# Reciprocal root of the head norms: two ScalarE activations instead of a ScalarE root and a VectorE reciprocal

## Chip, cores, metric

One core of a Trainium2 chip. The metric is the device time of one execution in microseconds (us); a change is judged by the median of several runs against the kernel before.

## What is computed

64 sequences of 128 tokens with 128 channels pass through a gated cross attention (16 heads of 8 channels, 120 context rows each), then through a gated block of causal self attention and four experts. The change sits in the self attention, in the norm of each query and key head:

```python
def _rms(x, w):
    return x * jax.lax.rsqrt(jnp.mean(x * x, axis=-1, keepdims=True) + EPS) * w
h = _rms(x, n1_w)
heads = lambda w_: (h @ w_.T).reshape(B, T, HEADS, HD).transpose(0, 2, 1, 3)
q = _rms(heads(wq), qn_w)        # HD = 8
k = _rms(heads(wk), kn_w)
```

The experts use GELU and SiLU, both attentions a softmax.

## The kernel before

The 64 sequences are worked off in 16 groups of four. A group passes five parts, one per step of a software pipeline: N (layer norm and projections of the cross attention), A (cross attention), B (projections and head norms of the self attention), D (self attention, gates, first expert layers), M (rest of the experts, output). So each step works on five groups at once. Four ramp steps fill the pipeline, a hardware loop runs the full step 12 times (t = 3 to 14), and four tail steps empty it.

What each engine does in a step is a list written out by hand (`SCHEDULE` and the ramp and tail lists); all five engine programs walk the same list and take from it only their own entries, in its order. No engine reorders: an instruction whose operand is late holds up all that its engine has behind it. Buffers and PSUM banks are guarded by semaphores; a bank counts one `filled` by the producer and one `drained` by the reader.

The entries around the change, in the order of the full step:

- ("B","squares"): GpSimd squares the queries and keys of a group; ("B","sums"): VectorE adds them by head into `hs`, 128 values per partition.
- ("A","base"), three product entries of D, ("D","nT",0): ScalarE copies `onT` (line 958).
- ("B","root"): ScalarE waits for `hs` and writes `hr`, the root of the mean square plus epsilon (line 905).
- ("M","e2_l2",0) and ("M","e2_l2",1): TensorE multiplies (line 1400), ScalarE applies Gelu (line 947). Between them ("D","wo",0): TensorE (line 1375), then VectorE adds into x2 (line 1147).
- ("B","scale"): VectorE waits for `hr`, takes the reciprocal (line 1070) and multiplies queries and keys by it (line 1072). It stands behind ("D","wo",0) on VectorE.
- estimate("A",3): TensorE (line 1305) fills four banks, VectorE takes their maxima (line 1091, out `mpadA`). values("D",3): TensorE (line 1362), ScalarE copies `oT` (line 955). ("M","e3_up",0) and (1) on TensorE and ScalarE.
- ("D","oT",1): TensorE transposes `oT` (line 1224), VectorE divides by the softmax sums (`rden` line 1130, `on` line 1132); ("D","nT",1): TensorE transposes `on`.
- later in the step ("B","qT") and ("B","kT"): transposes of the scaled queries and keys.

The exponentials of both attentions are line 951, those of the gates line 914; SiLU is made with Tanh (line 940). Ahead of some activations the trace shows an instruction ACT_TABLE_LOAD under the line of the activation behind it; the kernel's source doesn't write these.

In the third ramp step "root" stands between exponentials, in the fourth between a copy of `onT` and one of `oT`; in the last step that has it (t = 16) it stands ahead of the copy of `onT`.

Of the kernel before, what the change touches and what calls it, by code (L numbers as in the profile page):

```python
# [28 lines left out]
ACT = mybir.ActivationFunctionType  # L29
AX = mybir.AxisListType  # L30

P = 128
# [3 lines left out]
H = 16  # L36
HD = 8
# [4 lines left out]
G = 4  # L42
# [112 lines left out]
def slot_of(part, b, c):  # L155

    return (("AD".index(part) * G + b) * NT + c) % SLOTS
# [263 lines left out]
def build(nc, x, ctxT, weights, vcols, rows, out):  # L421
    ctx = ExitStack()
    with ctx:
        def sb(name, shape, dt=F32):
            return ctx.enter_context(nc.sbuf_tensor(name, shape, dt))

        def sem(name):
            return ctx.enter_context(nc.semaphore(name))
# [19 lines left out]
        rms_eps = sb("rms_eps", [P, G])  # L448
# [49 lines left out]
        rsA = sb("rsA", [P, G])  # L498
        rB = sb("rB", [P, 2, G])
        vrB = sb("vrB", [P, G])  # L500
        hs, hr = sb("hs", [P, 2 * H * G]), sb("hr", [P, 2 * H * G])
        ssM, msM, rM = sb("ssM", [P, G]), sb("msM", [P, G]), sb("rM", [P, G])
        lg = sb("lg", [P, 8, G, E])
        sm = sb("sm", [P, 5, G])
# [19 lines left out]
        a_stats, a_rstd, xn_ready, x1_base = (sem(n) for n in ("a_stats", "a_rstd", "xn_ready", "x1_base"))  # L524

        x1_copied, b_stats, b_pow, b_rs, hb_ready = (sem(n) for n in ("x1_copied", "b_stats", "b_pow", "b_rs", "hb_ready"))
        x2_ready, sq_ready, hs_ready, root_ready, hr_ready, qk_ready = (sem(n) for n in ("x2_ready", "sq_ready", "hs_ready", "root_ready", "hr_ready", "qk_ready"))
        y_ready = sem("y_ready")

        m_sq, m_ms, m_r, xf_ready, kept = (sem(n) for n in ("m_sq", "m_ms", "m_r", "xf_ready", "kept"))  # L530
# [22 lines left out]
        def half_of_maxima(p, half, b):  # L553

            at = (2 * half + b) * P
            return qd[p][M_ROW:M_ROW + 1, :, :, at:at + P].rearrange("p j c n -> p (j c) n").bitcast(F32)

        def half_source(p, half, b):

            return (mTl if half else mTr)[p][b * H:(b + 1) * H, :].bitcast(F32)  # L560

        def maxima_by_act(st, part, work):

            return (part, work, st.group(part, work)) in (("A", "mH", 0), ("B", "mH", 0), ("D", "mL", 0))
# [268 lines left out]
        def _(act):  # L833
# [8 lines left out]
            def clear_queries(p, first, last, done):  # L842

                nc.scalar.activation(qd[p][:, first:last].rearrange("p j c t -> p (j c t)"),
                                     one[:].to_broadcast([P, (last - first) * NT * TOK]), ACT.Copy, scale=0.0).then_inc(done, 1)
# [4 lines left out]
            def queries_or_keys(st, part, to, o, **affine):  # L850

                key = (part, {"N": o, "B": o + "T"}[part], 0)
                width = G * keys[to] if o == "k" else TOK
                bank = psum[st.bank[key]][:, 0:width]
                act.wait_ge(filled[st.bank[key]], st.fills(*key))
                nc.scalar.activation((qTb if o == "q" else kTb)[to][:], bank, ACT.Identity, **affine).then_inc(cast_ready[to], 1)
                n = uses_of_split(st, part)
                if not isinstance(n, int) or n > 0:

                    act.wait_ge(split_stored[o], n * USE_STORED)  # L860
                nc.scalar.activation(split[o][:, 0, 0:width], bank, ACT.Identity, **affine).then_inc(high_ready[o], 1)

            def step(st):
                for part, work, index in st.works:
                    key, g = (part, work, index), st.group(part, work, index)
# [31 lines left out]
                    elif (part, work) == ("B", "v"):  # L897
                        if st.first("B"):
                            act.wait_ge(vb_cleared, 1)
                        act.wait_ge(full, st.fills(*key))  # L900
                        nc.scalar.activation(V["B"][:, :, 0:HD],
                                             bank[:].rearrange("p (n d) -> p n d", d=HD), ACT.Copy).then_inc(done, 1)
                    elif (part, work) == ("B", "root"):
                        act.wait_ge(hs_ready, g + 1)
                        nc.scalar.activation(hr[:], hs[:], ACT.Sqrt, bias=rms_eps[:, 0:1], scale=1.0 / HD).then_inc(root_ready, 1)
                    elif (part, work) == ("B", "qT"):
                        if st.first("B"):
                            act.wait_ge(bias_ready, 3)
                        queries_or_keys(st, "B", "B", "q", scale=qns[:])
                    elif (part, work) == ("B", "kT"):  # L910
                        queries_or_keys(st, "B", "B", "k", scale=col["kn"])
                    elif (part, work, index) == ("D", "gates", 0):
                        act.wait_ge(gate_step, g * GATE_STEPS + 3)
                        nc.scalar.activation(lg[:, 3], lg[:, 2], ACT.Exp).then_inc(gate_exp, 1)
                    elif work == "mT":
                        act.wait_ge(full, st.fills(*key))
                        nc.scalar.activation(mTr[OP[part]][:], bank[0:G * H, 0:P], ACT.Copy).then_inc(done, 1)
                    elif work in HALVES:
                        p, half = OP[part], HALVES.index(work)
                        act.wait_ge(full, st.fills(*key))  # L920
                        nc.scalar.activation(mTl[p][:] if half else mTr[p][0:G * H // 2, :], bank[0:G * H // 2, 0:P],
                                             ACT.Copy).then_inc(done, 1)
                        if maxima_by_act(st, part, work):
                            if (part, work) == ("A", "mH"):
                                act.wait_ge(a_cleared, A_CLEARED)
                            elif (part, work) == ("B", "mH"):
                                act.wait_ge(b_cleared, B_CLEARED)
                            act.wait_ge(done, st.fills(*key))
                            for b in range(2):
                                act.dma_start(half_of_maxima(p, half, b), half_source(p, half, b)).then_inc(half_loaded[p][half], 16)  # L930
                        if st.parts == "N":
                            clear_queries("B", 0, HT // 2, b_cleared)
                    elif work == "fill" and index[0] == "e1_w1":

                        if index[1]:

                            for b, n in st.drains([("D", "fill", ("e1_w1", index[1] - 1))]):
                                act.wait_ge(drained[b], n)
                        act.wait_ge(full, st.fills(*key))
                        nc.scalar.activation(th, bank[:], ACT.Tanh, scale=0.5).then_inc(silu_tanh, 1)  # L940
                    elif work == "fill" and index[0] in HID_AT:
                        if index == ("e0_up", 0):

                            for b, n in st.drains([("D", "fill", ("e1_w1", 1)), ("D", "fill", ("e1_w2", 1))]):
                                act.wait_ge(drained[b], n)
                        act.wait_ge(full, st.fills(*key))
                        nc.scalar.activation(hid[:, HID_AT[index[0]] + index[1], :], bank[:], ACT.Gelu).then_inc(done, 1)  # L947
                    elif work == "s2":
                        k = keys[OP[part]]
                        act.wait_ge(full, st.fills(*key))  # L950
                        nc.scalar.activation(probs[0:k, slot_of(part, *index), :], bank[0:k, :], ACT.Exp,  # L951
                                             scale=SCALE if part == "A" else 1.0).then_inc(done, 1)
                    elif work == "pv" and key in st.bank:
                        act.wait_ge(full, st.fills(*key))
                        nc.scalar.activation(oT[:], bank[:], ACT.Copy).then_inc(done, 1)  # L955
                    elif work == "nT":
                        act.wait_ge(full, st.fills(*key))
                        nc.scalar.activation(onT[:], bank[:, 0:2 * P], ACT.Copy).then_inc(done, 1)  # L958

            run_steps(act, step)  # L960

        @block.vector
        def _(dve):
# [32 lines left out]
            def step(st):  # L996
                for part, work, index in st.works:
                    key, g = (part, work, index), st.group(part, work, index)
# [68 lines left out]
                            .then_inc(hs_ready, 1)  # L1067
                    elif (part, work) == ("B", "scale"):
                        dve.wait_ge(root_ready, g + 1)
                        nc.vector.reciprocal(hr[:], hr[:]).then_inc(hr_ready, 1)  # L1070
                        dve.wait_ge(hr_ready, g + 1)
                        nc.vector.tensor_tensor(
                            qk[:].rearrange("p b (h d) -> p (b h) d", d=HD), qk[:].rearrange("p b (h d) -> p (b h) d", d=HD),
                            hr[:].rearrange("p (n a) -> p n a", a=1).to_broadcast([P, 2 * H * G, HD]), ALU.mult)\
# [33 lines left out]
                    elif work == "fill" and index[0] == "down":  # L1108
                        e = index[1]
                        n = DOWNS.index(e)  # L1110
# [346 lines left out]
```

## Time and profile before

| | |
|---|---|
| median of 3 runs | 1075.44 us (1074.19 to 1075.52) |
| profiled execution | 1072.52 us, span 1070.7 us |
| TensorE | 1004.9 us busy, 94% of the span |
| VectorE | 789.2 us, 74% |
| ScalarE | 736.1 us, 69% |
| GpSimd | 337.8 us, 32% |
| granted TensorE clock, mean | 0.987 |
| table loads on ScalarE, by line | 836: 1, 905: 16, 914: 2, 947: 30, 951: 29 (78 in all; none at line 940) |

The shares are averages over the whole span. What a change in one place does is read from the chain of waits and from the timeline of that place. A step of the loop takes 62.7 us.

### The profile page before, as it was taken

Reading aid. Unit: us, or ns where it says so; the run is one execution under the profiler, and the core shown is the slowest. Engines: PE = TensorE matmul, PEld = TensorE weight load, DVE = VectorE, ACT = ScalarE, POOL = GpSimd, SP = SyncE. Lnnn points to the kernel's source line nnn. Section 1 sums busy time; section 2 is a strip of 40 time slices with the busy share of each in tenths; the row PEclk is TensorE's granted clock in tenths of the full one; section 3 lists DMA queues with packets and bytes.
Section 4 is the critical chain, followed back from the end, with each engine's and each line's share of the span. In section 5 each row is a group of like instructions: output and inputs, shape, how many; then the busy total and the mean of one; then the engine's idle time right before and its main releaser. Section 6 shows DMA issues by size and latency. Waiting matters only on the chain.

```text
span 1070.7 us, 26205 instructions
## 1 busy us (share of the span) xinstructions
PE 1004.9 (94%) x8649; PEld 626.3 (58%) x8649; DVE 789.2 (74%) x2172; ACT 736.1 (69%) x1334; POOL 337.8 (32%) x463
## 2 busy tenths in 40 slices
PE   6678799999999999999999999999999999999898
PEld 5445456566665656666565666656566665655565
DVE  8667777877787787778778777877877777774723
ACT  6466677676777767677776767777676777767453
POOL 5615134051513405151240515124051512404130
PEclk9989899999999999999999999999999999999999
DMA  7433432233343233434323343432234343221200
GB/s 233 134 106 130 136 112 93 90 102 127 115 142 111 90 92 103 127 115 140 109 92 92 106 127 115 136 109 93 90 111 127 115 135 109 82 67 62 69 1 20
DMA packets 77317, 114.28 MB, mean 107 GB/s; under 512 B 7776, under 2 KB 40160, under 8 KB 77152
## 3 DMA queue, kind: packets, MB, share of 16 engines
q1 hardware_dynamic: 76800, 111.53, 33.0%
q10 hardware_dynamic: 480, 2.26, 0.6%
q8 instruction: 23, 0.38, 0.1%
q14 instruction: 14, 0.11, 0.0%
HBM read 58.97 MB, written 53.74 MB: 105 GB/s over the span
## 4 chain that ended last, share of the span: by engine, by line
PE 64%; DVE 15%; ACT 11%; issue 7%; DMA 1%; SPq 1%; POOL 0%; DVEq 0%; ACTq 0%
PE ps_pv L1362 9%; PE ps_w L1388 9%; PE ps_s2a L1341 7%; PE ps_s2b L1341 5%; PE ps_s2a L1400 5%; PE ps_s2b L1407 4%; PE ps_t L1224 4%; ACT probs L951 4%; PE ps_w L1407 3%; DVE mpadB L1091 3%; PE ps_w L1273 3%; DVE mpadA L1091 3%; PE ps_t L1375 2%; PE ps_w L1224 2%; PE ps_w L1305 2%
## 5 line engine op out<-in xcount | busy, mean ns | idle before, releaser
L951 ACT ACTIVATE probs<-ps_s2a 120x512 f32<-120x512 f32 (+1 forms) x256 | 153.4, 599 | 73.1 <-PE ps_s2a L1341 64.7
L1091 DVE TENSOR_REDUCE mpadB<-ps_w 128x4 f32<-128x512 f32 x240 | 148.8, 684 | 24.9 <-PE ps_w L1305 24.9
L1091 DVE TENSOR_REDUCE mpadA<-ps_w 128x4 f32<-128x480 f32 x224 | 131.5, 651 | 38.0 <-PE ps_w L1305 38.0
L951 ACT ACTIVATE probs<-ps_s2b 120x512 f32<-120x512 f32 (+1 forms) x256 | 153.6, 600 | 0.0
L818 POOL TENSOR_SCALAR_AFFINE_SELECT probs<-probs 128x1024 f32<-128x1024 f32 x128 | 139.8, 1092 | 0.0
L1388 PE MATMUL ps_w<-W,hid 128*128 128x96 f32 x976 | 122.5, 279 | 1.0 <-DVE split_k L985 0.9
L1388 PEld LDWEIGHTS ps_w<-W,hid 128*128 128x128 f32 x976 | 114.9, 193 | 10.4 <-issue 4.9
L786 POOL TENSOR_TENSOR rB<-vrB,neg_half 128x4 f32<-128x4 f32 x16 | 16.1, 1007 | 207.2 <-DVE veB L978 207.2
L1341 PE MATMUL ps_s2a<-qdA,kstA 128*120 128x512 f32 x128 | 68.7, 537 | 7.0 <-ACT probs L951 3.1
L1400 PE MATMUL ps_s2a<-hid,W 128*128 128x512 f32 x152 | 74.4, 604 | 0.0
L1120 DVE SCALAR_TENSOR_TENSOR ym<-ps_w,gates,ym 128x96 f32<-128x96 f32 x184 | 45.7, 311 | 38.5 <-PE ps_w L1388 38.5
L955 ACT ACTIVATE oT<-ps_pv 128x512 f32<-128x512 f32 x64 | 38.2, 598 | 50.6 <-PE ps_pv L1362 50.6
L1341 PE MATMUL ps_s2a<-qdB,kstB 128*128 128x512 f32 x128 | 65.0, 508 | 7.4 <-ACT probs L951 1.9
L947 ACT ACTIVATE hid<-ps_s2a 128x512 f32<-128x512 f32 x73 | 43.7, 598 | 40.0 <-PE ps_s2a L1400 30.9
L1362 PE MATMUL ps_pv<-probs,VA 120*18 120x128 f32 x2048 | 68.5, 274 | 0.1
L1362 PE MATMUL ps_pv<-probs,VB 128*18 128x128 f32 x2048 | 68.5, 274 | 0.0
L1362 PEld LDWEIGHTS ps_pv<-probs,VA 120*18 120x18 f32 x2048 | 50.5, 98 | 23.4 <-issue 23.1
L817 POOL TENSOR_TENSOR tick<-one 128x1 f32<-128x1 f32 x128 | 24.9, 194 | 118.8 <-ACT probs L951 114.7
L1362 PEld LDWEIGHTS ps_pv<-probs,VB 128*18 128x18 f32 x2048 | 50.5, 97 | 17.1 <-issue 16.8
L958 ACT ACTIVATE onT<-ps_t 128x256 f32<-128x256 f32 x64 | 24.5, 383 | 50.4 <-PE ps_t L1224 50.4
L1341 PE MATMUL ps_s2b<-qdA,kstA 128*120 128x512 f32 x128 | 58.7, 458 | 0.0
L825 POOL TENSOR_TENSOR ym<-yb,one 128x128 f32<-128x128 f32 x16 | 6.4, 398 | 164.6 <-DMA out_x<-ym 164.6
(279 smaller groups left out, 2166.7 us busy)
## 6 DMA issues: line engine op xcount, KB each, us to landing
scratch_Aq<-split_q SPq DMA_DIRECT2D x48, 256.0 KB, 2.4
qdA<-scratch_Aq SPq DMA_DIRECT2D x64, 192.0 KB
scratch_Bq<-split_q SPq DMA_DIRECT2D x48, 256.0 KB, 2.4
scratch_Bk<-split_k SPq DMA_DIRECT2D x48, 256.0 KB, 2.9
qdB<-scratch_Bq SPq DMA_DIRECT2D x64, 192.0 KB
kstB<-scratch_Bk SPq DMA_DIRECT2D x64, 192.0 KB
scratch_Ak<-split_k SPq DMA_DIRECT2D x48, 240.0 KB, 2.3
kstA<-scratch_Ak SPq DMA_DIRECT2D x64, 180.0 KB
```

Of the source, the lines that this page charges most:

```text
L818: pool.affine_select(out=tile, in_=tile, compare_op=ALU.is_ge, fill=0.0, base=0, pattern=[[0, 2 * HT], [1, P]], channel_multiplier=-1).the ...
L947: nc.scalar.activation(hid[:, HID_AT[index[0]] + index[1], :], bank[:], ACT.Gelu).then_inc(done, 1)
L951: nc.scalar.activation(probs[0:k, slot_of(part, *index), :], bank[0:k, :], ACT.Exp, scale=SCALE if part == "A" else 1.0).then_inc(done, 1)
L955: nc.scalar.activation(oT[:], bank[:], ACT.Copy).then_inc(done, 1)
L1091: nc.vector.tensor_reduce(pair[:, :, c, b % 2] if halves else mneg[p][:, :, c, b], bank[:, 0:HT * k].rearrange("p (h k) -> p h k", h=HT), ...
L1120: ins = nc.vector.scalar_tensor_tensor(out=ym[:, b, KEEP:P], in0=bank[:, b * UP:(b + 1) * UP], scalar=gates[:, b, e:e + 1], in1=y[:, b, KE ...
L1224: ins = nc.tensor.transpose(psum[st.bank[key]][:, b * P:(b + 1) * P], of(b), identf[:])
L1341: mm(o, kst[p][:, c, b * k:(b + 1) * k], qd[p][:, :, c, b * P:(b + 1) * P], start=True, stop=True).then_inc(done, 1)
L1362: ins = mm(psum[st.bank[last]][32 * j:32 * j + VS, at:at + P], VB[p][0:k, first:first + VS], probs[0:k, slot_of(part, b, c), j * P:(j + 1) ...
L1388: ins = mm(bank[:, b * UP:(b + 1) * UP], hid[:, HID_AT[h] + k, b * P:(b + 1) * P], w[f"down{index[1]}"][:, k * UP:(k + 1) * UP], start=k = ...
L1400: ins = mm(bank[:], w[name][:, k * HID + c * P:k * HID + (c + 1) * P], hid[:, HID_AT[h] + k, :], start=k == 0, stop=k == chunks[-1])
L1407: mm(bank[:], w[name][:, c * P:(c + 1) * P], xfT[:], start=True, stop=True).then_inc(done, 1)
```

## The change

ScalarE takes the logarithm of the mean square plus epsilon into a new buffer `hl`, waits for its own result, and takes exp(-0.5 x) of it into `hr`. VectorE's reciprocal and its wait go; the multiplication follows directly on the wait for `hr`.

```diff
-        hs, hr = sb("hs", [P, 2 * H * G]), sb("hr", [P, 2 * H * G])
+        hs, hl, hr = (sb(n, [P, 2 * H * G]) for n in ("hs", "hl", "hr"))
...
                     elif (part, work) == ("B", "root"):
                         act.wait_ge(hs_ready, g + 1)
-                        nc.scalar.activation(hr[:], hs[:], ACT.Sqrt, bias=rms_eps[:, 0:1], scale=1.0 / HD).then_inc(root_ready, 1)
+                        nc.scalar.activation(hl[:], hs[:], ACT.Ln, bias=rms_eps[:, 0:1], scale=1.0 / HD).then_inc(log_ready, 1)
+                        act.wait_ge(log_ready, g + 1)
+                        nc.scalar.activation(hr[:], hl[:], ACT.Exp, scale=-0.5).then_inc(root_ready, 1)
...
                         dve.wait_ge(root_ready, g + 1)
-                        nc.vector.reciprocal(hr[:], hr[:]).then_inc(hr_ready, 1)
-                        dve.wait_ge(hr_ready, g + 1)
                         nc.vector.tensor_tensor(
```

The semaphore `hr_ready` is replaced by `log_ready`.

## Rows read from the trace of the kernel before

**Rows 1.** Page, chain that ended last, shares of the span by engine.

```profile
PE 64%; DVE 15%; ACT 11%; issue 7%; DMA 1%; SPq 1%; POOL 0%; DVEq 0%; ACTq 0%
```

**Rows 2.** Groups by line, ScalarE: count | busy us, mean ns | idle before us.

```profile
L951 ACT ACTIVATE probs<-ps_s2a 120x512 f32<-120x512 f32 (+1 forms) x256 | 153.4, 599 | 73.1 <-PE ps_s2a L1341 64.7 <-issue 1.2
...
L951 ACT ACT_TABLE_LOAD x29 | 37.2, 1283 | 0.5
...
L905 ACT ACT_TABLE_LOAD x16 | 20.5, 1283 | 0.3
...
L905 ACT ACTIVATE hr<-hs,rms_eps 128x128 f32<-128x128 f32 x16 | 6.4, 401 | 0.2
...
L914 ACT ACTIVATE lg<-lg 128x16 f32<-128x16 f32 x16 | 3.3, 209 | 0.8 <-DVE lg L1175 0.7
```

**Rows 3.** Line 1070 alone: duration ns min/median/max, first and last start us.

```profile
L1070 DVE RECIPROCAL hr<-hr x16: 941/942/953, 64.1 to 979.2; 128x128 f32<-128x128 f32 x16
```

**Rows 4.** Chain of waits in one loop step: start us, us on the chain, what.

```profile
356.89 0.36 DVE x L1147
357.25 0.87 DVE hr L1070
...
358.14 0.85 DVE qk L1072
...
359.28 2.21 DVE mpadA L1091 x4
...
361.54 0.36 DVE rden L1130
...
362.41 0.44 PE ps_t L1224 x2
```

**Rows 5.** Timeline of that step, ScalarE and TensorE: start us, us, instruction [idle before].

```profile
355.15 1.28 ACT L905 ACT_TABLE_LOAD   x1
...
356.87 1.28 ACT L947 ACT_TABLE_LOAD   x1
...
358.16 0.60 ACT L947 ACTIVATE hid<-ps_s2a 128x512 f32<-128x512 f32 x1
358.53 0.38 PE L1305 MATMUL ps_w<-kdA,qTbA 32*128 32x480 bf16 x4
...
359.84 1.12 PE L1400 MATMUL ps_s2a<-hid,W 128*128 128x512 f32 x2
359.97 0.60 ACT L955 ACTIVATE oT<-ps_pv 128x512 f32<-128x512 f32 x1 [0.73 <-PE ps_pv L1362]
360.80 0.60 PE L1224 MATMUL ps_t<-identf,oT 128*128 128x128 f32 x4
...
361.24 1.02 PE L1400 MATMUL ps_s2b<-hid,W 128*128 128x512 f32 x2
```

**Rows 6.** Timeline, same loop step and the one before: VectorE waiting for TensorE.

```profile
327.28 0.60 PE L1224 MATMUL ps_t<-identf,oT 128*128 128x128 f32 x4
...
327.91 0.36 DVE L1130 RECIPROCAL rden<-ps_t 128x32 f32<-128x32 f32 x1 [1.05 <-PE ps_t L1224]
...
343.60 0.38 PE L1305 MATMUL ps_w<-kdA,qTbA 32*128 32x480 bf16 x4
...
343.99 2.35 DVE L1091 TENSOR_REDUCE mpadA<-ps_w 128x4 f32<-128x480 f32 x4 [1.85 <-PE ps_w L1305]
```

**Rows 7.** Chain of waits, third ramp step.

```profile
62.40 1.28 ACT L905
...
65.11 1.24 DVE qk L1072
```

**Rows 8.** Chain of waits, fourth ramp step.

```profile
106.23 0.61 ACT oT L955
```

**Rows 9.** Last step with the change (t = 16): timeline, then chain of waits.

```profile
979.10 0.36 ACT L958 ACTIVATE onT<-ps_t 128x256 f32<-128x256 f32 x1
...
982.14 0.60 ACT hid L947
```

More of the change, by code:

```diff
@@ L526, in build @@
         x1_copied, b_stats, b_pow, b_rs, hb_ready = (sem(n) for n in ("x1_copied", "b_stats", "b_pow", "b_rs", "hb_ready"))
-        x2_ready, sq_ready, hs_ready, root_ready, hr_ready, qk_ready = (sem(n) for n in ("x2_ready", "sq_ready", "hs_ready", "root_ready", "hr_ready", "qk_ready"))
+        x2_ready, sq_ready, hs_ready, log_ready, root_ready, qk_ready = (sem(n) for n in ("x2_ready", "sq_ready", "hs_ready", "log_ready", "root_ready", "qk_ready"))
         y_ready = sem("y_ready")
```

## Prediction

> **What bounds the kernel now.** I read the page's chain first: two thirds of it are TensorE, the rest mostly VectorE and ScalarE in short pieces [rows 1]. So the kernel isn't bound by one engine's total but by TensorE's order with small gaps in it, and a change counts where it moves such a gap. Then the groups by line on ScalarE, which give the prices of table loads and activations [rows 2], and the reciprocal's own row [rows 3]. Then the chain of waits around one root in the loop [rows 4] and the timeline of the same place [rows 5]. The twelve loop steps and the step t = 15 have the same pattern to within some hundredths of a microsecond (I looked at seven of these 13), so one is worked out and multiplied by 13. The three other places with a root (third and fourth ramp step, t = 16) are read one by one [rows 7 to 9].
>
> In the loop step the reader is to see that the reciprocal and the multiplication by it lie on the chain: the addition of line 1147 at 356.89, the reciprocal from 357.25, the multiplication from 358.14, four maxima from 359.28, the division by the softmax sums from 361.54, and the transposes of `on` at 362.41 [rows 4]. But TensorE works through this stretch too. It fills the banks of the maxima from 358.53, multiplies for e3_up 0 from 359.84, transposes `oT` from 360.80 and multiplies for e3_up 1 from 361.24 [rows 5]. So the only gap of TensorE that this VectorE chain makes is the one ahead of 362.41, and it is small.
>
> **What goes on VectorE.** 16 reciprocals of 942 ns [rows 3], 15.1 us in all. In the loop step the multiplication could follow at 357.27 in place of 358.14, 0.87 us earlier, if `hr` is there by then. The first maximum then waits for TensorE: elsewhere line 1091 starts 0.39 us after the first matmul of line 1305 [rows 6], which here gives 358.53 + 0.39 = 358.92, 0.36 us earlier than 359.28. Four maxima end at 361.13. The division waits for the transposes of `oT`: 0.63 us after their start in [rows 6], so 360.80 + 0.63 = 361.43 in place of 361.54. That leaves 0.11 us for the transposes of `on`. TensorE can take it: the two matmuls of line 1400 end at 361.24 + 1.02 = 362.26 by the timeline, and groups overlap at their ends by some 0.16 us there (the transposes run from 360.80 to 361.40, the matmuls start at 361.24) [rows 5], so TensorE is free from about 362.10. Of 0.87 us taken off VectorE, 0.11 us reach the end of the step, 13 x 0.11 = 1.4 us in all. The rest is covered by TensorE's own work.
>
> **What comes on ScalarE, without the tables.** Ln takes the form of the root (128 columns, a bias from memory): 401 ns [rows 2]. The Exp behind it has 128 columns and no bias from memory. Its price isn't in the trace; it lies between the 16-column Exp of the gates at 209 ns and the root at 401 ns [rows 2]. The slope of ScalarE from this trace's wide activations puts it near 300 ns: 599 ns at 512 columns against 209 at 16 is 0.79 ns per column [rows 2], and 209 + 112 x 0.79 = 297. I take 0.30 us. The new wait on `log_ready` has behind it the Gelus of line 947 and the copy of `oT`; it costs a hop of 0.02 us, as between root and reciprocal today.
>
> **What happens to the tables.** This decides the sign. Each table load is 1.28 us [rows 2]. A loop step has five: root, Gelu, Exp, Gelu, Exp. Today the root stands behind the exponentials of part D and ahead of the Gelus, with a load ahead of it at 355.15 and one ahead of Gelu at 356.87 [rows 5]. The trace shows where functions share a table: Tanh, Copy and Identity stand behind Exp (and, in the tail, Tanh behind Gelu) without a load. It shows also where they don't: Sqrt after Exp, Gelu after Sqrt, Exp after Gelu each pay one. Ln occurs nowhere, so no row can say whether Ln and Exp stand in one table. The loads are placed function by function, immediately ahead of the first activation that misses its table; none of them shows that an earlier load was chosen for a function further on. Exp is now always served by a table that also served Tanh. If Ln brings a table of its own, as each of the three curves Exp, Sqrt and Gelu does, the order becomes load, Ln, load, Exp, load, Gelu: one load more than now. I take this as the likeliest, though only by a little.
>
> The Trainium skill speaks for the other way. "ScalarE: Activation LUTs", section "Table sets: the hidden batching unit", lists a set that holds both exp and ln and counts one load for ln followed by exp. "ScalarE activation tables: per-element evaluation and per-set limits", section "Table sets in the compiler and the runtime", says the loads are placed by the longest run that one set can serve. By that the change takes a load away rather than adding one, which is the second rival below. No row of this trace shows Ln, so the rule is neither borne out nor refuted.
>
> **The sum, with one load more.** Loop step on ScalarE: load to 356.43, Ln to 356.85, load 356.87 to 358.15, Exp 358.16 to 358.46, load to 359.76, Gelus at 359.78 and 360.27, copy of `oT` at 360.76, ending 361.36; today that copy ends at 360.57 [rows 5]. Everything behind the root moves by 1.28 + 0.30 = 1.6 us, of which 0.73 us is idle time ahead of the copy of `oT` [rows 5] and is absorbed. On VectorE the multiplication starts at 358.50 in place of 358.14, the maxima end near 361.85. On TensorE e3_up 0 needs the bank that the first Gelu frees at 360.38, so it starts at 360.42 (now 359.84); the transposes of `oT` start at 361.40, the division at 361.40 + 0.63 = 362.03 (now 361.54), and the transposes of `on` come 0.87 us behind it as now [rows 4], at 362.90: 0.48 us later than 362.41. So 13 x 0.48 = 6.2 us.
>
> Third ramp step: load 62.40 to 63.68, Ln to 64.10, load to 65.40, Exp to 65.71; the multiplication starts at 65.74 in place of 65.11 [rows 7], 0.6 us late on the chain. The exponentials behind it already pay a load today, so they lose only 0.3. Fourth ramp step: load and Exp (1.6 us) come ahead of the copy of `oT`, which moves from 106.23 [rows 8] to 107.43: 1.2 us. The load for the next exponentials goes, but TensorE waits there for the maxima's transfer, which has moved with it. Step t = 16: the copy of `onT` ends near 981.05 in place of 979.46 [rows 9]; line 1375, line 1400 and the second Gelu follow, that Gelu at 983.35 in place of 982.14: 1.2 us.
>
> Sum: 6.2 + 0.6 + 1.2 + 1.2 = 9.2 us. The profiled execution was 1072.52 us, the median of the runs 1075.44; the difference of 2.9 us is that between executions of one kernel, and I add the sum to the median: 1084.6 us. Bounds of this case: if Exp is nearer 209 or 401 ns each place moves by 0.1 us (1.6 us in all). If the late Gelus also hold e3_up 1, or the ScalarE backlog runs on into the transposes of the queries, a loop step loses 0.8 us instead of 0.48, 4 us more. If half of the loop's delay is taken up in later gaps, 3 to 4 us less. So 1079 to 1090 us.
>
> **Rivals.** *Ln's table also holds Exp, and it is loaded only when Ln comes* (chance 0.15). Then the root costs a load, Ln, Exp, and Gelu its load, as now. `hr` is there at 356.85 + 0.02 + 0.30 = 357.17, before VectorE has finished line 1147 at 357.25. The gelus move by 0.3 us, inside the 0.73 us of idle time ahead of the copy of `oT` [rows 5]. The loop gains 1.4 us as worked out; in the third ramp step the multiplication starts at 64.45 in place of 65.11, 0.7 us; the other two places gain nothing. Together 2.1 us: 1073.3 us, faster or no change about evenly. For it speaks that Tanh is found in more than one table; against it that no other curve of this kernel is.
>
> *The table with both functions is loaded at the start of part D's exponentials and serves them, Ln and Exp.* The chance is 0.22. A load goes in each step, 16 x 1.28 = 20.5 us of ScalarE's work [rows 2]. In the loop the multiplication still has to wait for line 1147, and TensorE doesn't wait for ScalarE between 355 and 361, so the gain is again 1.4 us. In the third ramp step Ln follows the exponentials directly and the multiplication comes when VectorE is free, near 63.85: 1.26 us. Together 2.7 us: 1072.7 us. It is what the longest-run rule of the Trainium skill cited above would do. This is the case on the other side of my forecast. It decides for faster as soon as one load serves Ln and Exp.
>
> *One load more, but the delay is hidden* (chance 0.06). If e3_up 0 were allowed its bank earlier or the backlog ended in the idle time of ScalarE, only the three single places would pay, some 3 us less the 1.4 us of the reciprocal: 1077 us. Against it: the copy of `oT` has 0.73 us of slack [rows 5] and 1.6 us come on top.
>
> **How the numbers follow.** The forecast has a chance of 0.57, the rivals 0.15, 0.22 and 0.06. A change of about 0.2% (2.2 us) is what a measurement of this kernel can tell from none. The first rival lies on this bound, the second a little beyond it, the third is near it on the slow side. Slower: 0.57 less a small part, plus a part of the third rival, 0.59. Faster: most of the second rival and a third of the first, 0.22. Same: 0.19. The range has to hold both signs: 1071.5 to 1090 us; the forecast's own range is 1079 to 1090.
>
> **What would show it.** The count of table loads decides first: 78 now. In the forecast they become 92 (one more in the 13 like steps and at t = 16; in the third and fourth ramp step the Exp of the root saves the load of the next exponentials). In the first rival they become 76, in the second 60 to 64. Next the start of the multiplication behind line 1147: directly behind it (0.02 us) in both rivals, 1.2 us later in the forecast. Next the idle time ahead of the copy of `oT`: gone in the forecast, 0.4 us or more otherwise. Last the start of the transposes of `on` after the addition of line 1147: 5.5 us now, 6.0 in the forecast, 5.4 in the rivals. The prediction is wrong if Ln and Exp share a load; its size is wrong if Exp or the Gelus' bank waits are off.

## The result

The changed kernel took 1087.39 us (median, 1084.63 to 1089.87) against 1074.82 us before; the ratio is 1.0118, 95% interval 1.0087 to 1.0148. On a second chip run it took 1082.57 us against 1074.11 us, ratio 1.0080 (1.0060 to 1.0100). So it is slower, by 8.5 to 12.6 us (0.8% to 1.2%). No load serves both Ln and Exp in this program: each of the 16 roots now pays two loads.

The groups by line of the changed kernel on ScalarE, with count, busy us, mean ns and idle before; the answer to [rows 2]:

```profile
L949 ACT ACT_TABLE_LOAD x30 | 38.5, 1283 | 0.6
L953 ACT ACT_TABLE_LOAD x27 | 34.6, 1283 | 0.5
L905 ACT ACT_TABLE_LOAD x16 | 20.5, 1283 | 0.3
L907 ACT ACT_TABLE_LOAD x16 | 20.5, 1283 | 0.3
L905 ACT ACTIVATE hl<-hs,rms_eps 128x128 f32<-128x128 f32 x16 | 6.4, 402 | 0.2
L907 ACT ACTIVATE hr<-hl 128x128 f32<-128x128 f32 x16 | 5.0, 309 | 0.2
```

With two loads for the gates and one at the start that makes 92, where there were 78. Line 953 (the softmax exponentials, line 951 before) has 27 in place of 29: in the third and fourth ramp step the root's Exp leaves its table standing for them. The Trainium skill ("ScalarE: Activation LUTs", section "Table sets: the hidden batching unit") counts one load for ln followed by exp; here the trace shows a load at each of the 16 Exps behind a Ln, and the measurement decides.

The page's chain by engine, the answer to [rows 1]: VectorE fell from 15% to 9% and ScalarE rose from 11% to 16%.

```profile
PE 63%; ACT 16%; DVE 9%; issue 9%; DMA 1%; SPq 1%; POOL 0%; ACTq 0%; DVEq 0%
```

One loop step of the changed kernel, chain of waits (start us, us, what), the answer to [rows 4]:

```profile
360.87 1.28 ACT L905
...
362.16 0.40 ACT hl L905
...
363.87 0.31 ACT hr L907
...
365.50 0.60 ACT hid L949
...
366.15 1.12 PE ps_s2a L1400 x2
367.27 0.59 PE ps_t L1224 x4
...
368.76 0.44 PE ps_t L1224 x2
```

And its timeline, the answer to [rows 5]:

```profile
362.60 0.36 DVE L1147 TENSOR_TENSOR x<-ps_t,x 128x192 f32<-128x192 f32 x1 [1.75 <-PE ps_t L1375]
...
364.20 1.28 ACT L949 ACT_TABLE_LOAD   x1
364.22 1.23 DVE L1072 TENSOR_TENSOR qk<-qk,hr 128x1024 f32<-128x1024 f32 x1 [1.26 <-ACT hr L907]
...
365.50 0.60 ACT L949 ACTIVATE hid<-ps_s2a 128x512 f32<-128x512 f32 x1
365.99 0.59 ACT L949 ACTIVATE hid<-ps_s2b 128x512 f32<-128x512 f32 x1
...
366.15 1.12 PE L1400 MATMUL ps_s2a<-hid,W 128*128 128x512 f32 x2 [0.53 <-ACT hid L949]
366.47 0.60 ACT L957 ACTIVATE oT<-ps_pv 128x512 f32<-128x512 f32 x1
367.19 0.42 PEld L1224 LDWEIGHTS ps_t<-identf,oT 128*128 128x128 f32 x4 [0.75 <-issue]
367.20 0.65 PE L1224 MATMUL ps_t<-identf,oT 128*128 128x128 f32 x4
...
367.89 0.36 DVE L1130 RECIPROCAL rden<-ps_t 128x32 f32<-128x32 f32 x1 [0.18 <-PE ps_t L1224]
```

The chain no longer runs through the multiplication and the maxima on VectorE; of VectorE's work only the division is left on it, and VectorE stands idle 0.18 us ahead of that, waiting for TensorE. It goes from the two loads of the root and the load of Gelu through the Gelu to the bank that e3_up 0 waits for: TensorE now stands idle 0.53 us ahead of it, where it had no idle time. The 0.73 us of slack ahead of the copy of `oT` [rows 5] are gone. The transposes of `on` come 6.16 us behind the addition of line 1147 in place of 5.52. From multiplication to multiplication a loop step takes (933.04 - 174.69) / 12 = 63.20 us; before it was (921.16 - 170.31) / 12 = 62.57 (the text ahead of the prediction gives it as 62.7). The rows at both ends of the changed kernel's twelve steps:

```profile
174.69 1.22 DVE L1072 TENSOR_TENSOR qk<-qk,hr 128x1024 f32<-128x1024 f32 x1 [1.26 <-ACT hr L907]
...
933.04 1.23 DVE L1072 TENSOR_TENSOR qk<-qk,hr 128x1024 f32<-128x1024 f32 x1 [1.26 <-ACT hr L907]
```

### The profile page after: what moved, and what is told of

The parts are those of the page before. It is cut to its first block, busy times and chain, and to the rows that moved or that the text cites. A ratio compares the mean times of both kernels' runs of the same rounds, so it can differ in the third digit from the quotient of the medians.

```text
span 1087.1 us, 26219 instructions
## 1 busy us (share of the span) xinstructions
PE 1013.0 (93%) x8649; PEld 629.1 (58%) x8649; DVE 776.6 (71%) x2156; ACT 756.3 (70%) x1364; POOL 338.5 (31%) x463
## 4 chain that ended last, share of the span: by engine, by line
PE 63%; ACT 16%; DVE 9%; issue 9%; DMA 1%; SPq 1%; POOL 0%; ACTq 0%; DVEq 0%
PE ps_pv L1362 9%; PE ps_w L1388 9%; PE ps_s2a L1341 7%; PE ps_s2b L1341 5%; PE ps_t L1224 5%; PE ps_s2b L1407 4%; PE ps_s2a L1400 4%; ACT probs L953 4%; PE ps_w L1407 3%; DVE mpadB L1091 3%; PE ps_w L1273 3%; PE ps_w L1224 2%; PE ps_w L1305 2%; PE ps_w L1301 2%; PE ps_t L1375 2%
## 5 line engine op out<-in xcount | busy, mean ns | idle before, releaser
L1375 PEld LDWEIGHTS ps_t<-W,onT 128*128 128x128 f32 x256 | 38.4, 193 | 33.8 <-issue 20.1
```

The lines of the kernel that those rows point to most:

```text
L1375: ins = mm(bank[:, s * n:(s + 1) * n], onT[:, s * P:(s + 1) * P], w["Wo"] if part == "A" else w["wo"], start=True, stop=True)
```

## The experiments

Periods below are always taken so, from the multiplication at t = 3 to the one at t = 15.

### The reciprocal alone

```diff
-                        nc.vector.reciprocal(hr[:], hr[:]).then_inc(hr_ready, 1)
-                        dve.wait_ge(hr_ready, g + 1)
```

> The kernel before with VectorE's reciprocal left out (queries and keys are multiplied by the root itself). ScalarE and its table loads are as before, 78. This prices the reciprocal alone. Theory (TensorE covers it): in the loop the transposes of `on` come 5.4 us behind the addition of line 1147 in place of 5.5, 13 x 0.11 = 1.4 us less, and about 1 us less in the third ramp step: 1072 to 1073 us. Rival (the reciprocal's 0.87 us on the chain is worth its whole length): 13 x 0.87 = 11 us less, 1063 us.

Measured: 1073.11 us against 1074.11, ratio 0.9992 (0.9977 to 1.0007). The loop step is (922.37 - 172.69) / 12 = 62.47 us, 0.10 us less than before. In this timeline the first maximum waits for TensorE, as worked out:

```profile
359.79 0.36 DVE L1145 TENSOR_TENSOR x<-ps_t,x 128x192 f32<-128x192 f32 x1 [1.75 <-PE ps_t L1373]
360.06 1.21 DVE L1070 TENSOR_TENSOR qk<-qk,hr 128x1024 f32<-128x1024 f32 x1
...
361.84 2.35 DVE L1089 TENSOR_REDUCE mpadA<-ps_w 128x4 f32<-128x480 f32 x4 [0.56 <-PE ps_w L1303]
...
363.70 0.60 PE L1222 MATMUL ps_t<-identf,oT 128*128 128x128 f32 x4
...
364.34 0.36 DVE L1128 RECIPROCAL rden<-ps_t 128x32 f32<-128x32 f32 x1
```

The rival of 11 us is excluded. 0.94 us of VectorE per step, 0.87 of them on the chain of waits, were worth 0.10 us. In the third ramp step the multiplication came 1.73 us behind the root's load (66.64 - 64.91) in place of 2.71, so the 1 us expected there was found. The time of the whole kernel shows neither: its interval goes from 2.5 us less to 0.8 us more.

### Two activations without a table load

```diff
-                        nc.scalar.activation(hl[:], hs[:], ACT.Ln, ...
+                        nc.scalar.activation(hl[:], hs[:], ACT.Exp, ...
```

> The changed kernel with Exp in place of Ln (the logarithm is left out), so that no table has to be loaded at the root at all. Same count of activations and the same wait on the own result as in the changed kernel; 60 to 64 table loads in place of 92. Theory (the table loads are the whole loss): 1072 to 1073 us, some 2.5 us under the kernel before, and the transposes of `on` 5.4 us behind line 1147. Rival (the second activation and the wait on the own result cost too, 0.3 us in each of 16 places): 1077 us or more.

Measured: 1072.10 us against 1074.11, ratio 0.9979 (0.9962 to 0.9996), with 60 loads. The loop step is (918.90 - 169.22) / 12 = 62.47 us, the same as without the reciprocal alone. So in the loop a second activation and its wait cost nothing where no load stands at the root, and a load less on ScalarE brings nothing there either. That the second activation is free behind two loads isn't shown by this; the next experiment bears on it. What separates this kernel from the changed one (10.5 us in these medians) is the table loads.

### One load more, reciprocal kept

```diff
                         nc.scalar.activation(hr[:], hs[:], ACT.Sqrt, ...).then_inc(root_ready, 1)
+                        nc.scalar.activation(atick[:], one[:], ACT.Exp)
```

> The kernel before (root and reciprocal kept) with an Exp of one column behind the root, whose result nobody reads. It adds a table load at 14 places, as the changed kernel does, without making `hr` later. Theory of the bank and the copy (the Gelus and the copy of `oT` come 1.5 us later and hold TensorE): about 0.5 us in each of 13 steps, 1080 to 1083 us. Rival (the loss comes through VectorE, whose multiplication starts 0.36 us later than before): the extra load behind the root would cost nothing, 1075 us.

Measured: 1081.98 us against 1074.11, ratio 1.0080 (1.0061 to 1.0100), the same ratio as the changed kernel beside it. The loop step is (928.36 - 170.84) / 12 = 63.13 us, 0.56 us more than before. This timeline shows VectorE's multiplication 2.99 us behind the root's load (360.35 - 357.36), exactly as before (358.14 - 355.15), and TensorE idle all the same:

```profile
357.36 1.28 ACT L906 ACT_TABLE_LOAD   x1
...
359.08 1.28 ACT L907 ACT_TABLE_LOAD   x1
...
360.35 1.22 DVE L1074 TENSOR_TENSOR qk<-qk,hr 128x1024 f32<-128x1024 f32 x1
...
360.58 1.28 ACT L949 ACT_TABLE_LOAD   x1
...
362.52 1.12 PE L1402 MATMUL ps_s2a<-hid,W 128*128 128x512 f32 x2 [0.41 <-ACT hid L949]
```

So the loss comes by the late Gelus and the late copy of `oT`, not by the late `hr`: 0.56 of the 0.63 us are there with `hr` in time. The remaining 0.07 us fit the root's Exp of 309 ns, where this kernel has one of 203; that isn't tested by itself. Nor is it separated which of the two, Gelu or copy, costs how much.

### The changed kernel again

> The changed kernel again, for a second profile and more times. The loop step took 63.20 us in its first profile and 62.57 before, 0.63 us more; the entry to the loop was 4.0 us late and the tail 4.3 us, with a granted clock of 0.67 between 70 and 80 us and of 0.52 between 1030 and 1040 us. Theory (the loop is the same in each execution, and what varies is the clock in ramp and tail): the loop step is again 63.2 us within 0.05, and the total goes with the mean clock, about 2 us less for 0.003 more. Rival (the loss in ramp and tail is fixed by the table loads): entry and tail are late by the same 4 us again whatever the clock.

Measured: 1082.57 us, ratio 1.0080 (1.0060 to 1.0100). The loop step is (933.39 - 174.85) / 12 = 63.21 us. The theory holds for the loop and for the tail. In the first profile TensorE stood idle 1.75 us before 1024.64 and ran mostly at its lower level of 1.2 GHz after it; in the second it stood idle for the same 1.75 us before 1025.03 and kept 2.4 GHz. The stretches (busy us and count of PE, PEld, DVE, ACT, POOL, then granted clock, DMA share, GB/s), first and second profile:

```profile
1030.00:1040.00 10.00, 9.54 (x79) 5.37 (x78) 0.00 (x0) 5.75 (x11) 6.03 (x10) 0.52 0.01 2
```

```profile
1030.00:1040.00 10.00, 9.49 (x117) 5.43 (x117) 0.78 (x2) 7.86 (x14) 7.62 (x13) 1.00 0.01 2
```

79 matmuls against 117 in the same time. From the multiplication at t = 16 to the end it was 94.2 us and 89.9 us. The entry to the loop, on the other hand, was as late as the first time (174.85 against 174.69), which speaks for the rival there. In the first four executions the mean clock and the time went together: 0.986 and 1084.63 us, 0.983 and 1085.80, 0.980 and 1088.99, 0.978 and 1089.87.

### Loop only, ramp and tail only

```diff
+                        if st.parts == PARTS:        # the second kernel: !=
                             ... Ln, wait, Exp
+                        else:
+                            ... Sqrt; and on VectorE the reciprocal
```

> Ln and Exp in the 12 loop steps only; root and reciprocal as before in the ramp and the tail. Theory (the loop step is 0.63 us longer whatever stands around it): 12 x 0.63 = 7.5 us over the kernel before, period of the loop 63.2 us. Rival (the loop carries less and the ramp's lost clock the rest): under 5 us over.

> Ln and Exp in the ramp and the tail only (4 places), root and reciprocal as before in the loop. Theory by the prediction's terms: 0.6 us at t = 15, 0.6 and 1.2 in the third and fourth ramp step, up to 1.2 at t = 16, together 3 to 3.6 us over the kernel before. Rival (where the changed kernel's first profile has 8 us in ramp and tail, a lower granted clock is part of every execution with the later root): 6 to 8 us over.

Measured: loop only 1081.42 us against 1075.13, ratio 1.0054 (1.0035 to 1.0072); ramp and tail only 1077.76 us, ratio 1.0024 (1.0005 to 1.0042). In microseconds 5.8 (3.8 to 7.7) and 2.6 (0.5 to 4.5), together 8.4, as the changed kernel has on the second run. For the loop the interval alone doesn't exclude the rival of under 5 us; the trace does. Between the root's loads of t = 3 and t = 15 lie 758.3 us in the first kernel (the multiplication of a step with Ln comes 3.35 us behind its first load, one with a root 2.99 us) and 750.7 us in the second; before it was 750.9, so the loop alone carries 7.4 us. For ramp and tail the rival of 6 to 8 us is excluded.

The loop-only kernel, whose ramp is that of before, had its multiplication of the fourth ramp step at 113.51 us, where before had 109.28 and the changed kernel 112.63. So the 4 us by which the changed kernel enters the loop late in its profile aren't the change's alone: the ramp varies by as much between executions, and before's profile was an early one.

### Matmuls in the ramp's idle times

```diff
+            BUSY = {(1, "B", "hT"): 34, (1, "B", "qT"): 24, (2, "B", "hT"): 16, (2, "N", "xT"): 40}
+                for _ in range(k):     # ahead of the wait for hb, qk or xn
+                    mm(psum[st.bank[key]][:, 0:P], identf[:], identf[:], start=True, stop=True)
```

> The changed kernel with matmuls whose result is overwritten, on TensorE in four idle times of the ramp (34 ahead of the first transposes of hb, 24 ahead of the first of the queries, 16 and 40 in the fourth ramp step), in the bank that is filled next. Theory (the spread between executions and the rest of the loss in the ramp are TensorE's clock after idle times): the granted clock stays at 1.0 between 50 and 130 us and the kernel is 3 to 6 us faster than the changed kernel, near 1078 us. Rival (TensorE isn't what the ramp waits for): no more than 1 us faster.

> The kernel before with the same matmuls in the idle times of the ramp (34, 20, 16 and 40). Theory (clock after idle times): 3 to 6 us faster than the kernel before, 1068 to 1071 us, and thereby faster than both kernels. Rival: within 1 us of the kernel before.

Measured: 1092.61 us for the changed kernel, 1081.19 us for the one before, ratios 1.0148 (1.0116 to 1.0179) and 1.0053 (1.0034 to 1.0072). The theory failed in both, and nobody had expected a loss: the kernels got slower, though their mean clock rose to 0.994 and 0.993. The chain of the kernel before with these matmuls shows why, they had become what everything waits for:

```profile
47.93 7.86 PE ps_w L1230 x68
```

34 calls are 68 instructions and 7.86 us, for an idle time of 4.4 us (4.43 ahead of the transposes of `hb` at 51.72 in the kernel before). Hence the same with about half the counts, 18, 10 (12 in the changed kernel), 8 and 20:

> The kernel before with fewer matmuls in the ramp's idle times (18, 10, 8 and 20 in place of 34, 20, 16 and 40): each call of 128 columns had taken 0.23 us, twice what was assumed, so that the larger counts ran 3.5, 2.2, 1.6 and 4.2 us past the operand they were to wait for. Theory (clock after idle times): now they end with the idle times, the granted clock stays near 1.0 from 50 to 130 us, and the kernel is 3 to 5 us faster than before, 1070 to 1072 us. Rival (the ramp waits on VectorE, ScalarE and transfers, not on TensorE's clock): within 1 us of before.

> The changed kernel with 18, 12, 8 and 20 such matmuls. Theory: 3 to 6 us faster than the changed kernel, 1077 to 1080 us, with less spread between executions, and 7.5 to 9 us over the kernel before with its own such matmuls, since the loop's loss of 0.63 us a step isn't one of clock. Rival: as slow as the changed kernel, 1082 to 1087 us.

Measured: the kernel before with the matmuls took 1069.73 us against 1073.50, ratio 0.9963 (0.9947 to 0.9979). That is 4.0 us less (2.3 to 5.7), as the theory had it, and beats both kernels. The changed kernel with them took 1082.97 us, ratio to before 1.0067 (1.0043 to 1.0091), which can't be told from the 1.0080 of its second run without them: here the rival came true. Stretches of the kernel before without them, and with them:

```profile
50.00:60.00 10.00, 7.33 (x33) 4.85 (x37) 1.12 (x4) 6.09 (x14) 3.23 (x3) 0.68 0.12 34
60.00:70.00 10.00, 6.92 (x78) 4.67 (x70) 7.03 (x21) 8.60 (x14) 2.19 (x3) 0.83 0.01 2
```

```profile
50.00:60.00 10.00, 8.59 (x74) 6.04 (x72) 1.72 (x5) 6.36 (x14) 4.53 (x4) 1.00 0.10 30
60.00:70.00 10.00, 7.10 (x70) 5.33 (x70) 7.48 (x23) 9.02 (x14) 1.40 (x2) 1.00 0.08 29
```

In the changed kernel with them the clock held up to 70 us and then fell: TensorE stood idle 2.67 us ahead of 71.14 and was granted 0.53 in the stretch from 70 to 80 us. Its timeline and stretch:

```profile
71.14 0.61 PE L1316 MATMUL ps_w<-causal_k,causal_q 32*128 32x512 bf16 x4 [2.67 <-DVE split_k L987]
...
73.24 1.91 PE L1377 MATMUL ps_pv<-probs,VA 120*18 120x128 f32 x32
```

```profile
70.00:80.00 10.00, 8.39 (x72) 4.40 (x76) 7.11 (x17) 2.56 (x6) 0.00 (x0) 0.53 0.84 272
```

The kernel before with them stood idle for the same 2.67 us at the same place and was granted 1.00 over 70 to 80 us:

```profile
70.27 0.40 PE L1316 MATMUL ps_w<-causal_k,causal_q 32*128 32x512 bf16 x4 [2.67 <-DVE split_k L985]
```

So the filling works as far as it reaches, and only if the clock isn't lost at the next idle time that is left. Why the kernel before kept it there in its profile and the changed one didn't isn't settled; the length of the idle time isn't the reason.

## Why the prediction was right

**The bound.** Right: TensorE's order with small gaps. It was the reading of TensorE beside the chain that priced the reciprocal. The chain alone gives 0.87 us a step, the timeline 0.11, and the kernel without it 0.10.

**The tables.** Right in sign and count: 92 loads forecast and found. The choice itself wasn't proven by any row of before. What stood for it were three curves with a table each and loads that looked no further than the next activation, and a chance of 0.57 was fair to that: that it came so was in part luck. Why Exp got a load of its own behind Ln, the trace doesn't say; it only shows the loads. The two rivals with a shared table fall with the count. The second one's time was priced rightly: the kernel without any load at the root, which has the 60 loads of that rival, measured 1072.10 us where the second rival had 1072.7.

**The Exp.** Estimated at 0.30 us between the bounds 0.21 and 0.40; measured 0.309.

**The loop step.** Mis-sized: 0.48 us forecast, 0.63 measured (63.20 against 62.57). The terms from the root's first load on: e3_up 0 forecast 5.27 us behind it, found 5.28; the copy of `oT` ends 6.21 us behind it, found 6.20; the transposes of `oT` were set 0.04 us behind the copy, and came 0.13 us behind it; the division was set 0.63 us behind the start of the transposes and came 0.69; the transposes of `on` were set 0.87 us behind it and came 0.87. The two hops make 0.14 to 0.15 us, the whole of the difference. The first could have been read before: TensorE loaded the weights of these transposes 0.12 us behind the end of the copy (360.69 - 360.57), as it does in the changed kernel (367.19 - 367.07).

```profile
360.69 0.47 PEld L1224 LDWEIGHTS ps_t<-identf,oT 128*128 128x128 f32 x4 [0.56 <-issue]
```

13 steps then give 8.1 us rather than 6.2.

**The third ramp step.** The multiplication was forecast 0.63 us late. It came 3.35 us behind the root's load (65.65 - 62.30) in place of 2.71 (65.11 - 62.40) [rows 7], so 0.64.

```profile
62.30 1.28 ACT L905
...
65.65 1.24 DVE qk L1072
```

**The fourth.** The copy of `oT` was forecast 1.2 us late, and the transposes behind it came 1.11 us late: 3.86 us behind the root's load (111.21 - 107.35) in place of 2.75 (106.88 - 104.13). The prediction let the next wait of TensorE, the one for the transferred maxima, move along with it. That wait took up part of the delay instead: it was 1.01 us before and is 0.72 now. The timelines of the kernel before and of the changed one:

```profile
104.13 1.28 ACT L905 ACT_TABLE_LOAD   x1
...
106.88 0.66 PE L1224 MATMUL ps_t<-identf,oT 128*128 128x128 f32 x4 [0.72 <-ACT oT L955]
...
111.06 0.75 PE L1341 MATMUL ps_s2a<-qdA,kstA 128*120 128x512 f32 x1 [1.01 <-issue]
```

```profile
107.35 1.28 ACT L905 ACT_TABLE_LOAD   x1
...
111.21 0.66 PE L1224 MATMUL ps_t<-identf,oT 128*128 128x128 f32 x4 [1.82 <-ACT oT L957]
...
115.09 0.75 PE L1341 MATMUL ps_s2a<-qdA,kstA 128*120 128x512 f32 x1 [0.72 <-issue]
```

Up to the matmul behind this wait 0.81 us are left (115.09 - 107.35 = 7.74 against 111.06 - 104.13 = 6.93).

**The step t = 16.** The second Gelu was forecast 1.2 us late; it came 6.11 us behind the root's load (995.69 - 989.58) in place of 4.64 (982.14 - 977.50), so 1.47. The copy of `onT` holds TensorE for 1.21 us:

```profile
989.58 1.28 ACT L905 ACT_TABLE_LOAD   x1
...
993.22 0.69 PE L1375 MATMUL ps_t<-W,onT 128*128 128x96 f32 x4 [1.21 <-ACT onT L960]
...
995.69 0.60 ACT L949 ACTIVATE hid<-ps_s2b 128x512 f32<-128x512 f32 x1 [0.61 <-PE ps_s2b L1400]
```

It reaches the end of the kernel. In the three profiles with a single load at the last root and a granted clock of 1.00 from 980 to 1050 us (without the reciprocal, loop only, and the kernel before with half the matmuls) the span ends 91.8 to 91.9 us behind that load; in the five with a second load there and the same clock (one load more, the changed kernel again, ramp and tail only, and the changed kernel with all and with half the matmuls) it ends 93.2 to 93.3 us behind it. The kernel before was at 93.2 in its own profile, with a clock of 0.83 from 1010 to 1020 us, and the changed kernel in its first at 97.5.

**The sum.** With the measured terms it is 8.1 + 0.6 + 0.8 + 1.5 = 11.0 us, where the forecast had 9.2 and the two runs had 12.6 and 8.5. The forecast of 1084.6 lies between 1082.57 and 1087.39, and the range held both; that it lies so near the middle is in part luck, as the loop's term was 1.9 us too small. What the prediction didn't have is the spread: ramp and tail move by some microseconds with TensorE's granted clock, in the same kernel, and the prediction named no term for that. In the tail these are the 97.5 us against 93.2. Whether the later root makes the lower clock more frequent can't be told from these runs.

**The rival of a hidden delay.** Excluded: 1.6 us met 0.73 us of slack ahead of the copy of `oT`, and TensorE stands idle 0.53 us for the late Gelu.

## What to carry to other kernels

An activation function is priced with its table: count which table stands when it comes and which must stand after it, and treat a table shared by two functions as unknown until a trace shows one load for both. An engine's time on the chain of waits isn't what its removal brings; look what the bound engine does in the same microseconds, here 0.94 us against 0.10. An engine with slack can carry only as much more as its next idle time, here 0.73 us; of what exceeds it most reaches the engine that waits for its buffers, here 0.63 of 0.87 us.

## Not expected

A call of a 128-column fp32 matmul is two instructions and takes 0.23 us (68 instructions in 7.86 us); I had assumed half. TensorE fell to its lower level behind an idle time in one execution and not in the next: after the same 1.75 us of idle time in the tail it was granted 0.52 over 1030 to 1040 us, or 1.00, and the group of 32 small matmuls of line 1362 takes 1.91 us at the lower level and 1.07 at the higher. Filling four idle times of the ramp brought 0.37% to the kernel before.
